# Local-attention stack: banks, orders of issue and the rotary table of one core's pipeline rearranged

## The reference, cut to what matters

```python
x = layernorm(x + mla_attention(x, ...))          # (4, 1024, 128), before the part that is changed
for i in range(6):                                # "local layers", on four sequences
    x = attn_layer(shift_tokens(x), Wqkv[i], ...) + x
    x = ffn_layer(shift_tokens(x), ...) + x
# attn_layer: 16 heads of 64, windows of 32 tokens that see themselves and the window before
qkv = x @ Wqkv                                    # 128 -> 3072
q = l2norm(q) * q_scale;  k = l2norm(k) * k_scale
q = q * cos * scale + rotate_half(q) * sin * scale        # rotary, by position
k = k * cos / scale + rotate_half(k) * sin / scale
out = softmax(mask(8 * q @ k_windows.T)) @ v_windows;  return out @ Wo
# ffn_layer
xn = layernorm(x) * g + b;  a, gate = split(xn @ W1 + b1)  # 341 wide each
return a * gelu(gate) @ W2 + b2
# finally
x = layernorm(x_first + x)
```

## Time and profile before

| what | value |
|---|---|
| time, median of 3 runs | 4713.65 us (4701.56 to 4717.32) |
| the profiled execution's own time | 4716.82 us, span 4715.0 us |
| mean granted TensorE clock | 0.955 of full speed |
| PE busy over the span | 88% |
| DVE, ACT, POOL busy | 62%, 56%, 59% |
| local layers | from about 925 us to 4670 us of the span |
| one round in the middle (qk_row issue to the next) | 2314.17 to 2468.93, about 153 us |

### The profile page before, as it was taken

The page is one execution under the profiler, slowest core; times in us unless marked ns, Lnnn a source line. Parts: engine busy times, 40 slices in busy tenths (PEclk is TensorE's granted clock), DMA queues, the critical chain, the costliest instruction groups (busy, mean ns, idle before and its releaser), DMA issues. The chain is left out here.

```text
span 4715.0 us, 163424 instructions
## 1 busy us (share of the span) xinstructions
PE 4152.8 (88%) x67078; PEld 2779.2 (59%) x67078; DVE 2916.5 (62%) x4217; ACT 2620.6 (56%) x4417; POOL 2778.1 (59%) x3434
## 2 busy tenths in 40 slices
PE   5878788689999999999999999999999999999994
PEld 2434344356666666666666666666666666666663
DVE  5565656466666666666666666666666666666664
ACT  2535354446556555665556565655666556665562
POOL 0000000177777777777777777777777777777771
PEclk8989798889999999999999999999999999999997
DMA  0000000112222222222222222222222222222222
GB/s 27 3 15 2 16 10 8 42 45 56 65 69 67 59 68 71 69 56 67 65 69 64 56 65 69 66 56 65 78 68 54 68 67 69 64 56 65 69 71 74
DMA packets 284548, 258.85 MB, mean 55 GB/s; under 512 B 122872, under 2 KB 258509, under 8 KB 271149
## 3 DMA queue, kind: packets, MB, share of 16 engines
q1 hardware_dynamic: 283820, 248.14, 19.7%
HBM read 117.63 MB, written 29.77 MB: 31 GB/s over the span
## 5 line engine op out<-in xcount | busy, mean ns | idle before, releaser
L785 DVE TENSOR_TENSOR products<-bank_d,table 128x1024 f32<-128x1024 f32 x772 | 937.9, 1215 | 711.9 <-ACT sq L612 696.2
L905 POOL TENSOR_TENSOR products<-products 128x2048 f32<-128x2048 f32 x192 | 870.9, 4536 | 282.9 <-DVE products L785 282.7
L411 PE MATMUL bank_d<-w_qkv,xT 128*128 128x512 f32 x1544 | 807.6, 626 | 21.5 <-DVE products L785 10.4
L612 ACT ACTIVATE sq<-bank_d 128x512 f32<-128x512 f32 x772 | 468.0, 606 | 482.9 <-PE bank_d L411 472.7
L942 POOL TENSOR_TENSOR qk_rot<-products,rnorm 128x2048 f32<-128x2048 f32 x192 | 695.4, 3622 | 14.9 <-POOL rnorm L924 14.6
L783 DVE TENSOR_REDUCE ss<-sq 128x16 f32<-128x1024 f32 x386 | 468.6, 1214 | 235.8 <-ACT sq L612 235.8
L949 POOL TENSOR_TENSOR prob<-prob,inv_sum 128x1024 f32<-128x1024 f32 x192 | 365.1, 1902 | 406.1 <-DVE inv_sum L765 406.1
L872 POOL MEMSET ident<- 128x128 f32 x1 | 0.2, 204 | 920.4 <-POOLq L1060 920.4
L1487 DVE TENSOR_REDUCE part_max<-s_max 128x1 f32<-128x512 f32 (+3 forms) x768 | 399.0, 554 | 152.6 <-PE s_max L1236 101.9
L457 PE MATMUL bank_a<-ident,qk_rot 128*128 128x128 f32 x3072 | 412.0, 290 | 70.5 <-issue 37.4
L457 PEld LDWEIGHTS bank_a<-ident,qk_rot 128*128 128x128 f32 x3072 | 366.4, 149 | 152.7 <-issue 105.1
(11 more groups left out here) (168 smaller groups left out, 7536.1 us busy)
## 6 DMA issues: line engine op xcount, KB each, us to landing
v_back<-v SPq DMA_DIRECT2D x96, 768.0 KB, 5.6
w_qkv<-in_Wqkv_dram SPq DMA_DIRECT2D x25, 1024.0 KB, 5.1
v_back<-v SPq DMA_DIRECT2D x192, 128.0 KB, 5.5
w_qkv<-in_Wqkv_dram SPq DMA_DIRECT2D x25, 512.0 KB, 5.4
xs<-x_layers SPq DMA_DIRECT2D x194, 64.0 KB, 2.1
w_o<-in_Wo_dram SPq DMA_DIRECT2D x24, 512.0 KB, 5.2
xr<-x_layers SPq DMA_DIRECT2D x96, 128.0 KB, 2.2
x<-x SPq DMA_DIRECT2D x96, 128.0 KB, 1.8
```

The costliest lines, as they stand in the source:

```text
L411: nc.tensor.matmul(bank[:, :], xT[:, P * a:P * (a + 1)], w_qkv[:, col:col + 512], start=True, stop=True).then_inc(d_filled if i < 8 else a ...
L612: nc.scalar.activation(sq[j % 2][:, 8 * c:8 * c + 8, :], bank_d[slot][:, :].rearrange("p (h d) -> p h d", d=DH), ACT.Square).then_inc(squa ...
L785: nc.vector.tensor_tensor(products[:, a, head:head + 8, :, :].rearrange("p h r (o d) -> p h r o d", o=2), bank[:, :].rearrange("p (h r d) ...
L905: link(nc.gpsimd.tensor_tensor(products[:, a, :, 0, :], products[:, a, :, 0, :], products[:, a, :, 1, :], ALU.add))
```

## The change

Six edits, all in `local_layers`:

1. q and k pieces are transposed and copied in the order 0, 1, 2, 3, 4, 6, 5, 7 (`QK_ORDER`), so that q and k of half 0 of tile 1 come before those of half 1; and the scores of half 0 wait for piece 6, those of half 1 for piece 7.
2. PE does `ffn_up` "aB" before chunk 9 and not after "gB".
3. ACT copies y (`yT`) before the second exponential and not after it.
4. PE does `ffn_down` before `times_v`; ACT's copy of its result (`y2T`) goes ahead of the attnT copies, and the bank order follows.
5. The rotary table is made in four parts, one at the end of each step on POOL.
6. `table_ready` counts parts; the waits of SP and DVE follow.

```diff
+QK_ORDER = (0, 1, 2, 3, 4, 6, 5, 7)
...
-        ring_a = Ring([(f"qk{i}", 1) for i in range(8)]
+        ring_a = Ring([(f"qk{i}", 1) for i in QK_ORDER]
                       + [v0, ("xn", 3), ("yT", 2), ("gA", 3), ("PT0", 1), ("PT1", 1), v1, ("gB", 3), v2,
-                         ("PT2", 1), ("PT3", 1), v3, ("xT", -1)]
-                      + [("O00", 1), ("O01", 1), ("O10", 1), ("O11", 1), ("y2T", 3)])
+                         ("PT2", 1), ("PT3", 1), v3, ("xT", -1), ("y2T", 3)]
+                      + [("O00", 1), ("O01", 1), ("O10", 1), ("O11", 1)])
...  (SP)
-                    sp.wait_ge(table_ready, s.f + 1)
+                    sp.wait_ge(table_ready, POS * (s.f + 1))
                     load_qk_rows(s.f + 1)
...  (PE)
             def score(s, pair, ph, half):
+                pe.wait_ge(a_free, ring_a.at(s, f"qk{6 + half}")[1] + 1)
                 if half == 0:
-                    pe.wait_ge(a_free, ring_a.at(s, "qk7")[1] + 1)
...
-                        transpose_qk(s, back1, 2 * i)
-                        transpose_qk(s, back1, 2 * i + 1)
+                        transpose_qk(s, back1, QK_ORDER[2 * i])
+                        transpose_qk(s, back1, QK_ORDER[2 * i + 1])
...
                     ffn_up(s, "aA")
+                    ffn_up(s, "aB")
                 project_now(9)
                 if runs(back3):
                     ffn_up(s, "gB")
-                    ffn_up(s, "aB")
...
                     transpose_x(s)
+                if runs(back3):
+                    ffn_down(s)
                 if runs(back1):
                     times_v(s, back1, 0)
...
                 project_next(2)
-                if runs(back3):
-                    ffn_down(s)
                 project_next(3)
...  (ACT: copy_qk in QK_ORDER too)
-                if runs(back1):
-                    exponentials(back1, 1)
                 if runs(back2):
                     bank = filled(s, "yT")
                     nc.scalar.activation(yT[:, :], bank[:, 0:PAIR], ACT.Copy).then_inc(a_free, 1)
+                if runs(back1):
+                    exponentials(back1, 1)
...
                     copy_x(s)
+                if runs(back3):
+                    bank = filled(s, "y2T")
+                    nc.scalar.activation(y2T[:, :], bank[:, 0:PAIR], ACT.Identity, ...).then_inc(a_free, 1)
                 if runs(back1):
                     copy_attnT(s, 0, 0)
...
                 square(new, 2)
-                if runs(back3):
-                    ... the same copy of y2T ...
                 square(new, 3)
...  (DVE)
-                if i == 0 and pair.p == 0:
-                    dve.wait_ge(table_ready, pair.f + 1)
+                if i == 0:
+                    dve.wait_ge(table_ready, pair.n + 1)
...  (POOL)
-            def make_table(f):
+            def make_table(f, p):
                 pool.wait_ge(qkrow_in, 16 * (f + 1))
+                rows = slice(2 * p, 2 * p + 2)
                 for sin, quarters in ((0, slice(0, 4, 3)), (1, slice(2, 0, -1))):
                     ins = nc.gpsimd.tensor_tensor(table[:, rows, :, quarters, :], rotary[:, rows, ...], ..., ALU.mult)
                 ins.then_inc(table_ready, 1)
...
-            make_table(0)
+            for p in range(POS):
+                make_table(0, p)
...
                     pool.wait_ge(d_free, chunk_at(now, 7)[1] + 1)
-                    if s.p == POS - 1:
-                        make_table(s.f + 1)
                     add_products(s, 1)
                     inverse_norms(1)
                     norm_qk(s, 1)
+                    make_table(s.f + 1, s.p)
```

## The result

The kernel became slower: 4800.45 us, the median of four runs (4786.56 to 4807.43), against 4710.41 for the kernel before (4701.56 to 4717.32). The ratio is 1.0186, with a 95% interval of [1.0165, 1.0207]. The prediction was 4626 with a range up to 4682. The profiled execution has a span of 4797.2 us, 82 more than before.

The account below looks back on a forecast made before the run. PE, busy 88% of the span, was taken as the bound, its waits as the gain. (-0.30 - 0.63) x 92 = -86 us, with -1 and -3 at the ends, gave 4627 profiled; forecast 4626, range 4580 to 4682.

Parts of the forecast that it names:

- The step that failed: First scores: 0.45 us saved becomes a DVE wait before phase 1's scores; counted 0, bounds 0 and -41 us.
- Rival B: Half given back: PE's instruction supply outrun, `times_wo` or `xn` late; +0.3 to +0.6 us a step, 4654 to 4680; chance 0.16.
- sign of failure: PE's waits with releaser "issue": growth by more than 1 us a round would show the forecast wrong.
- Edits 2 and 3: Around chunks 9 and 10: waits for yT and gates shrink; -0.3 us a step, bounds +0.60 and -0.81.
- Edit 4: Products with v: `ffn_down` fills their wait for v's last copy; -0.63 us a step.
- The table in four parts: POOL's end of step: parts of 1.45 us fit in about 2 us of idle cover; counted 0.
- Rival C: POOL becomes the bound if table parts cost by the instruction; PE waits for `xn`; 4873 us, chance 0.03.
- rival D: On ACT, the table load waits for the exponential, delaying gates and chunk 9 by 1.28 us; 4742 us, chance 0.04.
- The sum without edit 1: Local layers: gains around chunk 9 and before the products with v, plus the ends; -90 us, the rest counted 0.

Follow-up runs that it names:

- e5: The changed kernel plus one already met wait (piece 5) ahead of chunk 8: 4639.15 us, ratio 0.9858.
- e2: The changed kernel with q and k pieces in their old order and a single wait for the scores: 4623.81 us, ratio 0.9828.
- e3: The kernel before with only the new q and k order and a scores' wait for each half: 4758.75 us, ratio 1.0132.
- e1: The changed kernel with a single scores' wait, on piece 7, as before; the new piece order stays: 4620.1 us, ratio 0.9822.
- e6: The changed kernel with first scores waiting for piece 7, plus a met wait between the halves of phase 0's scores: 4625.91 us, ratio 0.983.
- e8: The kernel before with only "aB" ahead of chunk 9 and yT's copy ahead of the second exponentials: 4681.88 us, ratio 0.995.
- e7: The kernel before with only `ffn_down` ahead of the first `times_v`, y2T's copy and ring place moved: 4647.61 us, ratio 0.9872.
- e9: The kernel before with the "aB", yT and `ffn_down` moves, without the new q/k order and waits or the split table: 4629.79 us, ratio 0.9835.
- e11: The changed kernel with a single scores' wait and two met waits (pieces 5 and 4) ahead of chunk 8: 4640.45 us, ratio 0.985.

## Why the prediction was wrong

**The step that failed is edit 1, counted at 0 with bounds of 0 and -41 us.** Its reasoning on the semaphores was right: the 0.45 us before the first scores turned into a wait for DVE (0.37 in the row, 20.6 us in all, and 32.6 in e5). e2 and e3 show that the loss is edit 1's (177 us on the other edits, 50 alone), e1 that it is the two waits and not the order, e5 that one met wait ahead of chunk 8 takes nearly all of it away, e6 that a second wait between the halves does no such harm once that operation is back.

**Where the 170 us between the changed kernel and e1 lie**, by their profiled executions (4797.2 and 4627.4): PE's stops at L477 are 128.5 us more, and its busy time 39.6 us more (4167.1 against 4127.5), most of it `times_wo` (33) at the lower clock behind the stop. These make 168. The page's group of `times_wo`, in the changed kernel and in e1:

```profile
L491 PE MATMUL bank_a<-attnT,w_o 128*128 128x256 f32 x1536 | 385.6, 408 | 1.5 <-issue 1.5
...
L491 PE MATMUL bank_a<-attnT,w_o 128*128 128x256 f32 x1536 | 352.6, 383 | 1.7 <-issue 1.7
```

Other waits change places, with a sum near 0: DVE gets its row maximum late behind the stop in step 3, and PE then waits for a bank of DVE's products in 18 rounds (17.2 us, the last line of the waits shown above; e1 has no such line), while the wait for kT is gone.

**Rival B named what PE ran short of, and neither the reason nor the size.** It said that the fast stretches could outrun PE's supply of instructions, at +0.3 to +0.6 us a step. The measured price is 1.4 us a step at the stops alone (5.6 a round more than before), and the reason isn't a faster PE: in e1 and e2 PE has the same gain from edits 2 to 4, and its packets are in time in 60 and 59 of 66 steps. It is when the packet starts. The prediction's own sign of failure, "issue" grown by more than 1 us a round, is what came: it grew by over 5 (11.7 to 135.2 us at the scores, in 23 rounds).

**Edits 2 and 3** were given -0.30 us a step, -28 us; e8 measured -21. **Edit 4** was given -0.63, -58 us; e7 measured -55. Both steps were right, within the few us that these runs can tell.

**The table in four parts** was counted at 0 with 1.45 us a part; a part takes 1.43, and e9 against e2 shows no difference. Rival C has no support. POOL's idle time before its first sum is 2.27 in the row, not 0.6, since the step that covers it did not become shorter but longer.

**The table load behind an exponential** (rival D) starts 0.01 us behind it, and the gates start 0.02 behind the load, as behind a copy. The drain of 1.38 us, which the Trainium skill (ScalarE: Activation LUTs, What ACT_TABLE_LOAD costs) puts beside the load, shows in neither place.

**The sum without edit 1** was thus right: -90 us forecast, -85 (e2) and -89 (e1) measured. The forecast of 4626 us (by its own sum and the 3 us to the median it is 4624) is near the time of e1 and e2, 4620 and 4624. So the sum held for five of the six edits, and the kernel as it was changed was still outside the range.

**What stays open** is the rule by which a block is asked for early or late. The position of the wait for DVE doesn't give it: in PE's compiled program the wait is the same instruction number in e3 and e6 in every step, and the packet is in time in 14, 1 and 10 of 22 rounds of steps 1, 2 and 3 in the one and in 0, 19 and 22 in the other; e1 and the changed kernel differ there by one instruction. The number of operations ahead of that wait doesn't give it either (e6 in step 1, e11). e5 and e6 show that a single met wait turns a step from never in time to always (step 3, e5 against the changed kernel), or from mostly in time to never (step 1, e6 against e1); which property of the stream decides was not found.

Step 0 is late in all kernels here, and the records suggest why: its stop comes 264 matmuls and weight loads behind the start of phase 1's scores, where the wait for DVE stands, and those of steps 1, 2 and 3 come 232, 202 and 174 behind it. With blocks of 256, in step 0 even the block before the late one begins behind the wait. If a block is asked for only when the one before it has begun, step 0 can't be in time. No run tests this, and it doesn't explain steps 1 to 3 of the changed kernel.

## What to carry to other kernels

- A wait or a register operation added to an engine that is fed 16 KB of instructions at a time is not free because its semaphore is long met. When an edit moves one, compare the "issue" rows of the waits before and after, by line; a stop in the middle of a run of like matmuls, at the same matmul in every round, was a late packet of instructions here.
- Where such a packet is late, what stands on the DMA engines at that time can add to the stop: here a 1 MB load made 1.2 us into 3.8. Moving the load was worth 111 us in the kernel with late packets and nothing in the one without.
- To predict an edit that trades one wait for another with no gain in sight, give it a bound above nothing too: an edit worth 0 is not worth its risk. A better kernel is the change with the single wait for the scores, e1: 4620 us, 1.8% below the kernel before and 3.8% below the changed one.

## What the runs showed of the hardware

- A wait that never waits, put ahead of chunk 8, changed the time by 161 us of 4800 (e5).
- A packet of instructions took 0.9 to 1.4 us on its DMA queue in nine of ten cases of the changed kernel, and PE went on 1.2 to 1.6 us behind the end of a late one. In steps 1 and 2 the late packet started about 1.1 us behind the end of the wait at which PE stood.
- Before the first matmul of the loop's body PE stood for 2.7 us a round in the changed kernel (62.7 us in 23 rounds) and 2.9 in e1 (67.3). That it is the jump back is read from its place; no run tests it.
- A stop of 3.3 us, with the granted clock still at 1.00 in its first part, was followed by 6.1 us at a mean of 0.72; behind one of about 1 us no loss shows in `times_wo` (3.62 us).
